# The output stores of the last dense stage, moved from SyncE's queue to GpSimd's

## What is computed

```python
h = relu(layernorm(x))
x = x + L0(h)                                   # first layer, with a batch norm inside
h = relu(layernorm(x))
h2 = concatenate([h, agg, u[0]], axis=1)        # agg is zero where a node has no edge
x = x + relu(h2 @ W2a + b2a) @ W2b + b2b        # 50000 x 128, the output
```

## Time and profile before

| | us |
|---|---|
| median of 3 runs | 2328.08 |
| lowest and highest run | 2321.58, 2328.1 |
| the profiled execution | 2327.06 |
| its span | 2325.3 |
| the last dense stage in it | about 1437 to 1963 |

### The profile page before, as it was taken

One profiled execution on the slowest core, in us unless ns is written; L12 is line 12 of the kernel. 1 busy time (PEld: TensorE's weight loads), 2 busy tenths in 40 slices (PEclk: granted clock), 3 DMA queues, 4 the chain that ended last, 5 costly groups with the idle time before them and its releaser, 6 DMA issues. The chain is left out here.

```text
span 2325.3 us, 32089 instructions
## 1 busy us (share of the span) xinstructions
PE 1934.4 (83%) x7514; PEld 1098.4 (47%) x7514; DVE 1667.2 (72%) x3527; ACT 1313.6 (56%) x2509; POOL 1183.4 (51%) x919
## 2 busy tenths in 40 slices
PE   3699999988896898885565895799999996699887
PEld 2344444443332444443232332577777775355554
DVE  6599999967898999996234897677777773454543
ACT  3578888852222777774222222677777773565552
POOL 7456656428830433333885000545555552688885
PEclk9899999999898999998778897799999998899999
DMA  6678888744223999997343224999999994443441
GB/s 174 203 246 254 259 255 256 233 141 91 37 48 107 336 362 368 363 366 273 107 117 91 62 89 123 286 307 317 318 316 314 320 313 134 116 120 108 118 121 27
DMA packets 289511, 476.31 MB, mean 205 GB/s; under 512 B 85787, under 2 KB 162472, under 8 KB 289199
## 3 DMA queue, kind: packets, MB, share of 16 engines
q1 hardware_dynamic: 239100, 441.09, 59.8%
q0 software_dynamic: 46400, 33.03, 7.0%
q10 hardware_dynamic: 3824, 0.13, 0.1%
HBM read 272.11 MB, written 202.60 MB: 204 GB/s over the span
## 5 line engine op out<-in xcount | busy, mean ns | idle before, releaser
L388 POOL DMA_INDIRECT first_x<-in_x,first_index x200 | 261.2, 1306 | 174.9 <-ACT first_xn L581 88.3
L999 POOL TENSOR_TENSOR last_xh<-last_xin,last_hin 125x512 f32<-125x512 f32 x100 | 127.2, 1273 | 222.1 <-DMA last_xin<-in_x 222.1
L783 POOL DMA_INDIRECT second_entry<-node_map,second_si x100 | 129.2, 1292 | 198.2 <-DVE second_src_row L798 170.2
L1074 PE MATMUL last_psH<-last_g,W2a 128*128 128x500 f32 x400 | 189.9, 598 | 25.5 <-DVE last_hid L1036 25.4
L1083 PE MATMUL last_psO<-W2b,last_hid 128*125 128x128 f32 x1600 | 190.9, 273 | 0.0
L1083 PEld LDWEIGHTS last_psO<-W2b,last_hid 128*125 128x125 f32 x1600 | 182.5, 188 | 0.9 <-issue 0.9
L1117 POOL DMA_INDIRECT elast_x<-x_rows,elast_si x100 | 129.9, 1299 | 75.0 <-issue 61.3
L202 ACT ACTIVATE last_xn<-last_x,last_nb,last_rstd 125x128 f32<-125x128 f32 x400 | 163.9, 487 | 0.4 <-DVE last_nb L1030 0.4
L1125 POOL DMA_INDIRECT out<-elast_o,elast_ends x100 | 135.2, 1352 | 45.6 <-issue 45.0
L541 PE MATMUL first_psW<-first_h,W_in 128*128 128x500 f32 x300 | 153.5, 594 | 0.0
L1117 POOL DMA_INDIRECT att_rows<-h_rows,att_idx x100 | 130.3, 1303 | 35.7 <-issue 28.4
(11 more groups left out here) (278 smaller groups left out, 5067.1 us busy)
## 6 DMA issues: line engine op xcount, KB each, us to landing
hT<-first_h SPq DMA_DIRECT2D x100, 250.0 KB
yT<-first_y SPq DMA_DIRECT2D x100, 250.0 KB
second_yin<-yT SPq DMA_DIRECT2D x50, 500.0 KB
second_hin<-hT SPq DMA_DIRECT2D x50, 500.0 KB
yT<-second_y SPq DMA_DIRECT2D x50, 500.0 KB
last_yin<-yT SPq DMA_DIRECT2D x50, 500.0 KB
first_x<-in_x SPq DMA_DIRECT2D x100, 224.0 KB
h_rows<-second_rows SPq DMA_DIRECT2D x50, 448.0 KB
```

The lines of the kernel that those rows point to most:

```text
L388: pool.indirect_dma_start(x[:, to % X, j], None, a["x"], bass.IndirectOffsetOnAxis(index[:, end, r % 2, j:j + 1], 0), bounds_check=NODES - ...
L783: pool.indirect_dma_start(entry[:, q], None, scratch.node_map, bass.IndirectOffsetOnAxis(si[:, q], 0), bounds_check=NODES - 1, oob_is_err= ...
L999: pool.tensor_tensor(xh[:, q % 4], xin[:, q], hin[:, q], ALU.add).then_inc(m.xh, 1)
L1074: last = pe.matmul(psH[h][:, 0:CH], w.W2a[:, 0, h * 128:(h + 1) * 128], g[:, q % 2], start=True, stop=True)
```

## The change

`store_o` leaves SyncE's list and joins GpSimd's with a lag of 13 chunks. It runs at the odd chunks only and stores the same pair in the same two DMAs. The semaphores of these stores now start at zero instead of 16, so `make_o` doesn't wait in its first round, and SyncE's last waits count accordingly.

```diff
-        o_stored, o_stored2 = ph.stored("o_stored", 4), ph.stored("o_stored2", 4)
+        o_stored, o_stored2 = ph.loaded("o_stored", 4), ph.loaded("o_stored2", 4)
...
-                def store_o(t, q, r):
-                    hold(sp, ph.seen, m.o, made(2 * t + 1))
-                    dst = pair_rows(out, t * 2 * CH)
-                    sp.dma_start(dst[0:SPLIT], pair(o, q)[0:SPLIT]).then_inc(o_stored[q], 16)
-                    sp.dma_start(dst[SPLIT:TILE], pair(o, q)[SPLIT:TILE]).then_inc(o_stored2[q], 16)
-
...
-                unrolled(NCHUNK // 2, U // 2, [(0, load), (2, edges(load_edges, 2)), (4, store_x1), (6, edges(store_edges, 2)), (9, store_o)])
+                unrolled(NCHUNK // 2, U // 2, [(0, load), (2, edges(load_edges, 2)), (4, store_x1), (6, edges(store_edges, 2))])
...
-                unrolled(NCHUNK, U, [(0, add_h2), (5, add_bias)])
+                def store_o(k, q, r):
+                    if k % 2 == 0:
+                        return
+                    t, s = k // 2, k // 2 % (U // 2)
+                    hold(pool, ph.seen, m.o, made(k))
+                    dst = pair_rows(out, t * 2 * CH)
+                    pool.dma_start(dst[0:SPLIT], pair(o, s)[0:SPLIT]).then_inc(o_stored[s], 16)
+                    pool.dma_start(dst[SPLIT:TILE], pair(o, s)[SPLIT:TILE]).then_inc(o_stored2[s], 16)
+
+                unrolled(NCHUNK, U, [(0, add_h2), (5, add_bias), (13, store_o)])
...
-                    dve.wait_ge(o_stored[q // 2], 16 * r + 16)
-                    dve.wait_ge(o_stored2[q // 2], 16 * r + 16)
+                    if r > 0:
+                        dve.wait_ge(o_stored[q // 2], 16 * r)
+                        dve.wait_ge(o_stored2[q // 2], 16 * r)
```

More of the change, by code:

```diff
@@ L952, in _ @@
                 for q in range(U // 2):
-                    for sems in (x1_stored, x1_stored2, o_stored, o_stored2):
-                        sp.wait_ge(sems[q], 16 + 16 * len(range(q, NCHUNK // 2, U // 2)))
+                    stores = len(range(q, NCHUNK // 2, U // 2))
+                    for sems in (x1_stored, x1_stored2):
+                        sp.wait_ge(sems[q], 16 + 16 * stores)
+                    for sems in (o_stored, o_stored2):
+                        sp.wait_ge(sems[q], 16 * stores)
             @block.scalar
```

## The result

| | before | after |
|---|---|---|
| median, us (14 runs each) | 2328.09 | 2340.76 |
| lowest and highest, us | 2319.59, 2333.74 | 2330.76, 2360.42 |
| the profiled execution, us | 2327.06 | 2338.57 |
| its span, us | 2325.3 | 2336.8 |

The changed kernel is slower: the ratio is 1.0057, with a 95% interval of 1.0039 to 1.0076, which is 13.3 us (9.1 to 17.7). 2330 us was forecast, from 2306 to 2350.

A forecast was written before the change was run, and what follows sets the result against it. The prediction took the DMA engines to bound the last dense stage. Terms of 0 + 0 + 0 + 1.6 + 1 = +2.6 us on the profiled 2327.06 us gave 2329.7, forecast as 2330 us, range 2306 to 2350.

The forecast's parts named there:

- The bound: Last dense stage, steady 400 us: bound by DMA engines at share 1.05, with TensorE 22 us behind.
- Rival A: Steady stage: DMA rate rises until TensorE bounds, its `last_hid` wait below 8 us; 2306 to 2321 us, chance 0.33.
- The price of a byte on q0: Steady-stage stores of `out`: a byte costs the same as on q1, 0 us taken, between -22 and +50.
- B: Rival: steady-stage bytes on q0 are dearer than on q1, +13 to +50 us, 2343 to 2380; chance 0.26.
- GpSimd's issue cost: Steady stage: two DMAs cost GpSimd 3.1 us a pair, fitting its 4.5 us idle; 0 us taken.
- The new wait: GpSimd's `store_o` waiting for `make_o`, 13 steps behind: met over 7 us before it is reached, 0 us.
- The step on GpSimd's added work: Two DMAs behind GpSimd's additions delay the odd chunk's `add_h2`; its waiter `make_x1` has 14 us of cover; 0 us.
- The order: Stores come about one pair earlier, so one more lies ahead of the last loads: +1.6 us, between 0 and 3.3.
- The end of the stage: Last two stores issued on GpSimd 2.2 us later at most; +1 us taken.
- C: Rival: GpSimd becomes the bound in the steady stage if two DMAs exceed 4.5 us; +42 us, 2372; chance 0.05.

The follow-up runs named there:

- e10: Kernel before, all stores on SyncE, with GpSimd adding two 256-byte DMAs a pair into an unread tile; ratio 1.0036 to the kernel before.
- e2: Kernel before with only the last pair of output rows stored by GpSimd, 49 pairs staying on SyncE; ratio 1.0006 to the kernel before.
- e4: Changed kernel with `last_nb` and `last_eh` given one SBUF input each, leaving out the last layer norm's mean; ratio 1.0038 to the kernel before.
- e5: Kernel before with `last_nb` and `last_eh` given one SBUF input each, leaving out the last layer norm's mean; ratio 0.9982 to the kernel before.
- e6: Changed kernel with the first 34 pairs stored by GpSimd and the last 16 by SyncE; ratio 1.0001 to the kernel before.
- e3: Changed kernel with all 50 stores issued by ScalarE on its own queue q10, same lag of 13 chunks; ratio 0.9986 to the kernel before.
- e9: Changed kernel with the first 16 pairs stored by SyncE and the last 34 by GpSimd; ratio 1.0017 to the kernel before.
- e8: Kernel before, stores on SyncE, with GpSimd given one more 125x512 addition a pair into an unread tile; ratio 1.0016 to the kernel before.

## The prediction against the runs

- **The bound.** Right: DMA share 1.05 in both, TensorE's last link 23.5 us where about 22 was named, 83 chunks in 400 us. Rival A asked for under 8 us there and falls. Nor did a freed SyncE give anything: it was the full queue that held it. With two DMAs less in nine the small load of `last_xin` took 1.89 us to issue (median) in place of 1.04.
- **The price of a byte on q0.** Taken as q1's own; it is 0.66 points a MB against 0.85. Right in that B falls, and the ratios above 1 in the earlier trace rows did not carry over from scattered rows to contiguous ones. The cheaper bytes brought no time back either: the rate was 318 GB/s for 313 in the steady stretch, but the stage did not get shorter, and e10 has 318 GB/s with every store on q1.
- **GpSimd's issue cost.** Mis-sized in the safe direction, 3.1 us a pair taken for a measured 1.27; hidden, as said. Idle time ahead of `last_xh` went from 4.6 to 149.4 / 41 = 3.6 us a pair, not to 1.5, for the same reason.
- **The new wait.** 0, right. The row of GpSimd waiting for `last_o` (14.3 us, 3 times) is not it: at those places the instruction behind is an addition with no store ahead of it, and e2, with no store of GpSimd in the stretch, has such a row of 6.3 us, 2 times.
- **What was not in the sum: VectorE.** The step on GpSimd's added work named who waits for GpSimd, and not who is held while GpSimd is busy. The hold-up was worth 61 us of VectorE's time in 400. As far as e4, e5 and e6 can tell it does not make the difference between the two kernels; that was luck, not a step of the argument.
- **The order.** The mechanism was right and the size short: 1.6 us for one store ahead of the last loads, between 0 and 3.3. The traces have 0.9 to 1.4 MB, about two pairs, so 3 to 4.5 us if each byte costs what the rate says, which e3 puts in doubt. The step's own count gives 9 - 6.5 - 1.2 = 1.3 pairs and was rounded down to one. It also took the moment of issue for the moment of moving: if a store on q1 stood behind the 12 us of backlog that the earlier trace rows show for a load, the 7.7 us on q0 are another half pair. Together an estimate of 1.75 pairs, 0.9 MB.
- **The end of the stage.** This is the step that failed: +1 us, from "2.2 us later at most", against 6.2 measured. It timed the two DMAs and took the stage to be over when they had landed. That part is right: SyncE's wait for the landings ended at 1964.9 us for 1961.6 before, with the last `last_o` 2.2 us later, which leaves 1.1. GpSimd's own drain of 9.0 us was not in it. The row for it, 1.36 us for a queue that had issued no DMA since the attention stage, stood in the trace of before. So did drains at the ends of the stages with 100 or 200 indirect DMAs of GpSimd. Their rows are 6 to 21 us long, of which 2.1 to 4.6 us are left when the last of these DMAs has been issued: enough for a term, though not for one of 8. Neither was looked at. With 6.2 for 1 and 3.8 for 1.6 the same sum gives 2337 us, 0.4% over before, a forecast of slower.

So the range held the time and the side was wrong: 0.57% slower, where the likeliest case was no change. The slower cases had been given 0.31, and for two mechanisms (B and C) that both fell.

## What to carry to other kernels

When DMAs move to GpSimd's queue, look at GpSimd's drain at the end of the stage, not only at their landing: it grew from 1.4 to 9 us here and is free only where GpSimd is done well ahead of the last engine. Let another queue take the last few transfers (three pairs of fifty were enough to hide it). Expect that a transfer on its own queue passes a backlog; in a stage bound by bytes the loads may have to pay for a store that goes early, though the runs here don't settle by how much. And a busy time that grows on an engine without new work is worth explaining, but cost it by taking it away from both kernels before it is believed.

## What the runs showed of the hardware

- A drain of GpSimd's sequencer ends 0.1 us after its last instruction with no DMA of its own in the stage, 2.7 us after two, 5.6 to 5.7 us after 68 and 8.2 us after 100, whether they carried 250 rows a pair or 256 bytes each (8.3 us), and whether the last was issued just before or 105 us before (e9, e6).
- A plain DMA costs GpSimd 0.70 us for 2 x 112 rows, 0.57 for 2 x 13, 0.50 for one piece of 256 bytes and 1.16 for 2 x 125, with no gap behind it; an indirect one of 125 rows 1.27 us and 0.30 of gap.
- A small VectorE operation with two SBUF inputs can be held through several GpSimd instructions in a row: 3.47 us for one that takes 0.16. The holds over 1.3 us are in the kernels where GpSimd issues DMAs in between (after 3.47, e10 3.00; before 1.28, e8 1.21).
- Moving stores from a full queue to another one moved about 1 MB of them ahead of loads, once, at the place of the switch.
